# A fused attention and expert layer on one core: the context of four heads is turned by a DMA transpose instead of by TensorE

## The reference

```python
xn = _layernorm(x, axis=-1)
x = x + attention(xn, qkv_w, out_w, bias_p, bias_a, rope_freqs) + experts(xn, Wg, w1, w2)
```

```python
attn = jax.nn.softmax(scores + kb[None], axis=-1)
out = jnp.einsum('bhqk,bhkd->bhqd', attn, v)
out = out.transpose(0, 2, 1, 3).reshape(Bb, Ss, H * D)
return out @ out_w.T
```

## Time and profile before

| | before |
|---|---|
| median of 3 runs | 1443.87 us (1440.41 to 1444.68) |
| span of the profiled execution, first to last instruction | 1431.5 us |
| PE matmul busy | 1271.8 us (89%) |
| DVE busy | 1109.8 us (78%) |
| ACT busy | 1036.1 us (72%) |
| POOL busy | 696.1 us (49%) |
| mean granted TensorE clock | 0.945 of 2.4 GHz |

### The profile page before, as it was taken

How to read it: one execution, slowest core, us unless ns; L and a number is a source line. 1 busy time by engine, 2 the same in 40 slices (tenths; PEclk the granted TensorE clock), 3 DMA queues, 4 the chain that set the end, 5 groups by cost and what they waited for, 6 DMA issues and landing times.

```text
span 1431.5 us, 38280 instructions
## 1 busy us (share of the span) xinstructions
PE 1271.8 (89%) x13668; PEld 967.7 (68%) x13668; DVE 1109.8 (78%) x2166; ACT 1036.1 (72%) x1859; POOL 696.1 (49%) x536
## 2 busy tenths in 40 slices
PE   5622999995799999989998998999999999999996
PEld 5621888882477677767776776777677767777764
DVE  6873999973588887868886887788787868888885
ACT  3773888852688788768777787778688767877874
POOL 3064000004556666646655656566466646655600
PEclk8565999999899999999999999999999999999999
DMA  8554666621222223222312321132223212211220
GB/s 270 202 177 134 207 234 220 220 103 32 65 82 55 53 78 93 61 48 69 82 46 48 97 54 47 46 103 64 55 63 93 60 48 75 76 46 46 82 53 16
DMA packets 103602, 132.50 MB, mean 93 GB/s; under 512 B 17138, under 2 KB 89855, under 8 KB 103408
## 3 DMA queue, kind: packets, MB, share of 16 engines
q1 hardware_dynamic: 91136, 109.72, 26.4%
q0 software_dynamic: 4352, 12.41, 2.8%
q10 hardware_dynamic: 7920, 7.87, 1.7%
HBM read 58.79 MB, written 21.00 MB: 56 GB/s over the span
## 4 chain that ended last, share of the span: by engine, by line
PE 53%; ACT 7%; issue 7%; DVE 7%; SPq 1%; DVEq 1%; ACTq 0%; DMA 0%
PE ps_t L1294 13%; PE ps_x L1249 11%; PE ps_o L1319 8%; PE ps_s L1282 6%; PE ps_s L1283 6%; PE ps_x L1269 5%; ACT prob L1085 3%; DVE neg L1187 3%; PE ps_x L1259 3%; ACT ot_hi L1071 2%; DVE yacc L1172 1%; ACT pt_hi L1066 1%; SPq L963 1%; DVE yacc L1138 0%; DVE ctxt L1162 0%
## 5 line engine op out<-in xcount | busy, mean ns | idle before, releaser
L1144 DVE SCALAR_TENSOR_TENSOR pt_lo<-ps_t,pt_hi 128x1024 f16<-128x1024 f32 x256 | 312.6, 1221 | 155.2 <-ACT pt_hi L1066 155.2
L1187 DVE CUSTOM_DVE_ANT_0 neg<-ps_s,strips,score_scale 128x512 f32<-128x512 f32 x512 | 362.1, 743 | 31.9 <-PE ps_s L1283 28.1
L1085 ACT ACTIVATE prob<-neg,neg_max 128x512 f32<-128x512 f32 x512 | 362.9, 713 | 8.1 <-DVE neg_max L1187 8.1
L1066 ACT ACTIVATE pt_hi<-ps_t 128x1024 f16<-128x1024 f32 x256 | 262.0, 1023 | 113.4 <-PE ps_t L1294 113.0
L1014 POOL TENSOR_TENSOR parts<-rot,parts 128x1024 f16<-128x1024 f32 x62 | 132.2, 2134 | 307.5 <-ACT parts L1060 307.5
L1294 PE MATMUL ps_t<-ident,prob 128*128 128x128 f32 x2048 | 270.2, 274 | 3.8 <-ACT prob L1085 3.7
L1294 PEld LDWEIGHTS ps_t<-ident,prob 128*128 128x128 f32 x2048 | 236.5, 142 | 37.6 <-issue 9.3
L1282 PE MATMUL ps_s<-qk 128*128 128x512 f16 x512 | 198.1, 387 | 33.2 <-issue 18.4
L1319 PE MATMUL ps_o<-val_hi,pt_hi 128*128 128x64 f16 x2048 | 206.2, 193 | 14.5 <-DVE ctxt L1162 12.7
L1319 PE MATMUL ps_o<-val_hi,pt_lo 128*128 128x64 f16 x2048 | 206.2, 193 | 0.0
L1319 PE MATMUL ps_o<-val_lo,pt_hi 128*128 128x64 f16 x2048 | 206.2, 193 | 0.0
(11 more groups left out here) (186 smaller groups left out, 2518.9 us busy)
## 6 DMA issues: line engine op xcount, KB each, us to landing
raw<-in_L_ffn_w_dram SPq DMA_DIRECT2D x32, 1024.0 KB, 6.7
qk<-parts SPq DMA_DIRECT2D x512, 64.0 KB
kswap<-qk SPq DMA_DIRECT2D x64, 256.0 KB
xa<-in_L_attn_x_dram SPq DMA_DIRECT2D x8, 512.0 KB, 6.9
xt_dram<-xth SPq DMA_DIRECT2D x8, 512.0 KB, 5.1
slots_dram<-zeros SPq DMA_DIRECT2D x4, 1024.0 KB, 8.4
xa<-slots_dram SPq DMA_DIRECT2D x16, 256.0 KB, 5.1
expert_dram<-xa POOLq DMA_DIRECT2D x16, 256.0 KB, 6.3
```

The lines of the kernel that those rows point to most:

```text
L1066: nc.scalar.activation(pt[0][:, (l - 1) % 2].rearrange("p q k c -> p q (k c)"), ps_t[item % 2][:], ACT.Copy, scale=P_SCALE).then_inc(turne ...
L1085: nc.scalar.activation(prob[:, l % 2, q, :], neg[:, l % 2, q, :], ACT.Exp, bias=neg_max[:, 2 * (l % 2) + q:2 * (l % 2) + q + 1], scale=-1. ...
L1144: nc.vector.scalar_tensor_tensor(out=pt[1][:, (l - 1) % 2].rearrange("p q k c -> p q (k c)"), in0=ps_t[item % 2][:], scalar=P_SCALE, in1=p ...
L1187: nc.vector.tensor_tensor_reduce(neg[:, l % 2, q, :], ps_s[q][:], strips[:, h, start:start + S], score_scale[:, 0:1], 3.0e38, ALU.add, ALU ...
```

## The change

The context is no longer transposed by PE. `read_context` writes two heads (half a group) into a `ctxt` of half the size; ACT makes a float16 high part of it straight from SBUF (`context_hi`, at k = 2 and k = 6), DVE the low part (`context_lo`, at k = 3 and k = 7), both into `ctx_parts`. When both halves of a group are there, SP issues one DMA transpose of 128 x 2048 float16 values (512 KB, sixteen squares of 128 x 128) into `ot`. PE waits for it before the y fill at k = 6. In the program of SP `turn_context(b, j - 1)` comes before the `xcur` load and the `move` of the same j, and behind the `move` of the j before. To make room, `prod` shrinks to two slices, and POOL now writes two of the four products into `rot` and combines in place; the number and shapes of POOL's operations stay.

```diff
-        prod = sb("prod", [P, 4, S])
+        prod = sb("prod", [P, 2, S])
...
-        ctxt = sb("ctxt", [P, TPB, HG * D])
-        ot = [sb(f"ot_{n}", [P, 2, S], F16) for n in ("hi", "lo")]
+        ctxt = sb("ctxt", [P, TPB, P])
+        ctx_parts = sb("ctx_parts", [P, 2, 2, TPB, P], F16)
+        ot = sb("ot", [P, 2, 2, S], F16)
...
+            def turn_context(b, j):
+
+                group = 4 * b + j
+                wait(sp, filled, y_fills(b, j))
+                sp.sem_inc(went_on)
+                sp.wait_ge(ctx_lo, 2 * group + 2)
+                sp.sem_inc(went_on)
+                sp.dma_start_transpose(ot[:].rearrange("p a k (t c) -> p (a k t) c", t=TPB),
+                                       ctx_parts[:].rearrange("p a k t c -> p (a k t c)")).then_inc(ctx_turned, 16)
...
                 for j in range(4):
+                    if j or not is_first(b):
+                        turn_context(b, j - 1)
                     if j == 1 and not is_last(b):
...
+            turn_context(NB - 1, 3)
...
-                for i, (half, table) in enumerate(((0, cos), (1, sin), (0, sin), (1, cos))):
-                    nc.gpsimd.tensor_tensor(prod[:, i, :], proj[:, w, half, :], table[:], ALU.mult).then_inc(turned_parts, 1)
+                wait(pool, parts_lo, 2 * F - 1 + w)
+                for half, tables in enumerate(((cos, sin), (sin, cos))):
+                    nc.gpsimd.tensor_tensor(rot[:, w, half, :], proj[:, w, 0, :], tables[0][:], ALU.mult).then_inc(turned_parts, 1)
+                    nc.gpsimd.tensor_tensor(prod[:, half, :], proj[:, w, 1, :], tables[1][:], ALU.mult).then_inc(turned_parts, 1)
...
-            def ctx_hi(b, item):
-                act.wait_ge(turned, items(b, item))
-                nc.scalar.activation(ot[0][:], ps_t[item % 2][:], ACT.Copy, scale=1.0 / P_SCALE).then_inc(turned_hi, 1)
+            def context_hi(b, l):
+
+                unit = PAIRS // 4 * b + (l - 6) // 4
+                two = (l - 6) // 4 % 2
+                act.wait_ge(ctx_read, unit + 1)
+                if not two:
+                    wait(act, ctx_turned, 8 * unit)
+                act.sem_inc(went_on)
+                nc.scalar.activation(ctx_parts[:, 0, two], ctxt[:], ACT.Copy, scale=1.0 / P_SCALE).then_inc(ctx_hi, 1)
...
-                if k == 3 and not (is_first(b) and j == 0):
-                    ctx_hi(b, 9 * j + 4)
+                if l % 4 == 2 and not (is_first(b) and l == 2):
+                    context_hi(b, l)
...
+            def context_lo(b, l):
+
+                unit = PAIRS // 4 * b + (l - 6) // 4
+                two = (l - 6) // 4 % 2
+                dve.wait_ge(ctx_hi, unit + 1)
+                nc.vector.scalar_tensor_tensor(out=ctx_parts[:, 1, two], in0=ctxt[:], scalar=1.0 / P_SCALE, in1=ctx_parts[:, 0, two],
+                                               op0=ALU.mult, op1=ALU.subtract).then_inc(ctx_lo, 1)
...
-                if k == 3 and not (is_first(b) and j == 0):
-                    ctx_lo(b, 9 * j + 4)
+                if l % 4 == 3 and not (is_first(b) and l == 3):
+                    context_lo(b, l - 1)
...
-            def context_transposes(b, item, units):
-                wait(pe, turned_lo, items(b, item - 2))
-                pe.wait_ge(ctx_read, units)
-                for kt in range(2):
-                    for t in range(TPB):
-                        last = nc.tensor.transpose(ps_t[item % 2][:, kt, t * P:(t + 1) * P],
-                                                   ctxt[:, t, kt * P:(kt + 1) * P], ident[:])
-                last.then_inc(turned, 1)
...
                     if kind[0] == "y" and k == FILLS:
-                        pe.wait_ge(turned_lo, items(b, 9 * j + 4))
+                        pe.wait_ge(ctx_turned, 16 * (4 * b + j))
                     fill(kind, b, l, fills_before(b, l))
                 if l or not is_first(b):
                     transposes(b, l)
-                if k == 3 and not (is_first(b) and j == 0):
-                    context_transposes(b, 9 * j + 4, PAIRS // 4 * b + 2 * j)
```

More of the change, by code:

```diff
@@ L902, in fills_before, with pairs_turned, y_fills @@
             return n
[L904 to L912, removed]
+        def pairs_turned(b, l):
+            return PAIRS * b + l
+        def y_fills(b, j):
+            return fills_before(b, 8 * j + 8)
         def wait(eng, s, v):
@@ L1001, in turn, with rotate, low @@
                 wait(pool, turned_parts, done)
-                for i, (half, table) in enumerate(((0, cos), (1, sin), (0, sin), (1, cos))):
-                    nc.gpsimd.tensor_tensor(prod[:, i, :], proj[:, w, half, :], table[:], ALU.mult).then_inc(turned_parts, 1)
-                pool.wait_ge(turned_parts, done + 4)
-                wait(pool, parts_lo, 2 * F - 1 + w)
-                nc.gpsimd.tensor_tensor(rot[:, w, 0, :], prod[:, 0, :], prod[:, 1, :], ALU.subtract).then_inc(turned_parts, 1)
-                nc.gpsimd.tensor_tensor(rot[:, w, 1, :], prod[:, 2, :], prod[:, 3, :], ALU.add).then_inc(turned_parts, 1)
+                wait(pool, parts_lo, 2 * F - 1 + w)
+                for half, tables in enumerate(((cos, sin), (sin, cos))):
+                    nc.gpsimd.tensor_tensor(rot[:, w, half, :], proj[:, w, 0, :], tables[0][:], ALU.mult).then_inc(turned_parts, 1)
+                    nc.gpsimd.tensor_tensor(prod[:, half, :], proj[:, w, 1, :], tables[1][:], ALU.mult).then_inc(turned_parts, 1)
+            def rotate(F, w):
+                done = 6 * (2 * F + w)
+                pool.wait_ge(turned_parts, done + 4)
+                nc.gpsimd.tensor_tensor(rot[:, w, 0, :], rot[:, w, 0, :], prod[:, 0, :], ALU.subtract).then_inc(turned_parts, 1)
+                nc.gpsimd.tensor_tensor(rot[:, w, 1, :], rot[:, w, 1, :], prod[:, 1, :], ALU.add).then_inc(turned_parts, 1)
+            def low(F, w):
+                pool.wait_ge(parts_hi, 2 * F + w + 1)
+                nc.gpsimd.tensor_tensor(parts[:, 1, w], rot[:, w], parts[:, 0, w], ALU.subtract).then_inc(parts_lo, 1)
             def step(F, fills):
-                turn(F, 0, fills + 2)
-                turn(F, 1, fills + 4)
                 for w in range(2):
-                    pool.wait_ge(parts_hi, 2 * F + w + 1)
-                    nc.gpsimd.tensor_tensor(parts[:, 1, w], rot[:, w], parts[:, 0, w], ALU.subtract).then_inc(parts_lo, 1)
+                    multiply(F, w, fills + 2 * w + 2)
+                    rotate(F, w)
+                for w in range(2):
+                    low(F, w)
             def gather(b, j):
@@ L1083, in slot @@
                     if q == 0:
-                        wait(act, turned, items(b, pair_item(l - 1)))
+                        wait(act, turned, pairs_turned(b, l - 1))
                     nc.scalar.activation(prob[:, l % 2, q, :], neg[:, l % 2, q, :], ACT.Exp,
@@ L1119, in _ @@
             pair_hi(NB - 1, PAIRS)
-            ctx_hi(NB - 1, 37)
+            context_hi(NB - 1, PAIRS + 2)
         @block.vector
@@ L1157, in read_context @@
                 dve.wait_ge(pv_done, PAIRS * b + l - 2)
-                if not two:
-                    wait(dve, turned, items(b, 9 * (l // 8) + 4))
                 nc.vector.reciprocal(rsum[:], sums[:, two, :]).then_inc(chain, 1)
                 dve.wait_ge(chain, unit + 1)
-                nc.vector.tensor_tensor(ctxt[:, :, two * P:two * P + P].rearrange("p t (h d) -> p h t d", h=2),
+                nc.vector.tensor_tensor(ctxt[:].rearrange("p t (h d) -> p h t d", h=2),
                                         ps_o[:].rearrange("p (h t d) -> p h t d", h=2, t=TPB),
@@ L1288, in transposes @@
                 s = PAIRS * b + l
-                item = pair_item(l)
-                wait(pe, turned_lo, items(b, item - 2))
+                wait(pe, turned_lo, pairs_turned(b, l - 2))
                 for q in range(2):
@@ L1293, in transposes @@
                     for kt in range(TPB):
[L1294 removed]
+                        last = nc.tensor.transpose(ps_t[l % 2][:, q, kt * P:(kt + 1) * P],
                                                    prob[:, (l - 1) % 2, q, kt * P:(kt + 1) * P], ident[:])
[L1296 to L1304 removed]
                 last.then_inc(turned, 1)
```

28 lines of the change are left out of this document (10 added, 18 removed).

## The result

| | before | after |
|---|---|---|
| median of 20 runs | 1438.24 us (1432.27 to 1445.94) | 1448.78 us (1435.65 to 1458.50) |
| ratio, 95% interval | | 1.0055 (1.0029 to 1.0080) |
| span of the profiled execution | 1431.5 us | 1439.0 us |
| time of that execution | not listed | 1440.67 us |
| mean granted TensorE clock there | 0.945 | 0.956 |

The changed kernel is slower by 0.55%, about 8 us by the ratio. +57 us were forecast: the sign was right and the size seven times too large. The measured time lies inside the range of 1425 to 1680, and under the forecast's own range of 1460 to 1600.

A forecast was written before the change was run, and what follows sets the result against it. Attention was taken as bound by PE, busy 89%. Batches +41 us, clock +12 and tail +4 gave +57 on 1443.87, about 1500 us; own range 1460 to 1600, 8-in-10 range 1425 to 1680.

The forecast's parts named there:

- The direction: Whole kernel: the change makes it slower, chance 0.75.
- SP is still inside the `move`: SP's program: in groups 1 to 3 the transpose's issue is bound by SP, 1.1 us after the kswap issues end.
- the landing: Transpose into ot, from issue to landing: 6.5 us, taken between 4.3 and 9.0; landing of 5 to 10 us, chance 0.52.
- a short piece costs the same: Upper bound of landing: 256-byte pieces cost 49 ns like 1 KB packets, 6.3 us of moving, 9.0 us in all.
- my own sum: PE at slot 6, groups 0 to 3: -0.6, +3.7, +1.8, +0.2 us; +41 us over the stream, +57 with clock and tail.
- Rival A: Slot 6: the transpose lands like a plain copy, 1432 us, faster; sign turns at about 5.0 us landing; chance 0.25.
- Rivals B and C: B: squares issued one by one, 12.6 us landing, 1731 us, chance 0.15; C: squares strictly serial, about 2010 us, 0.08.
- The clock term: PE idle 6 us at slot 6 of group 1 lowers its clock: 1.5 us each in 8 groups, +12 us.
- The aftermath goes: Slots 4 and 5: 0.2 + 0.4 us extra behind the PE transposes vanish in each group; DVE's piece takes 0.75 us.
- The tail: At the end, ctxt done to first y fill grows from 4.3 to 8.1 us: +4 us.
- GpSimd's edit: POOL's four products wait for the previous step's low parts, which POOL itself finished earlier: zero cost.
- The base: Profiled span 1431.5 us plus 12.4 us around it gives the 1443.87 us median to which +57 us is added.

The follow-up runs named there:

- runs 1 and 3: Changed kernel with SP's transpose issued ahead of the kswap DMAs; the first also shortens ScalarE's wait, 1404.19 us; the second keeps it, 1401.97 us.
- run 9: Early transpose with old ScalarE wait, plus a second transpose of the 256 KB high half right behind it into an unread tile: 1408.64 us, one run.
- run 4: Changed kernel with a plain copy of the same 512 KB in place of the transpose: 1421.34 us, ratio 0.9897 to the kernel before.
- run 7: Changed kernel with the transpose ahead of kswap and the low part on GpSimd, 1/16384 multiplied in while ps_o is read: 1392.14 us, ratio 0.9667.
- run 8: Kernel before with only GpSimd's part of the change (prod of two slices, two products written into rot): 1441.78 us, ratio 1.0020.
- run 3: Changed kernel with the transpose ahead of the kswap DMAs, ScalarE's wait left as it was: 1401.97 us, ratio 0.9735 to the kernel before.

## Why the prediction was right and wrong, by its own steps

**The direction was right, and so was the place.** "SP is still inside the `move`" is what the trace shows. The transposes of the batch read above were forecast at 22.8 us of group 1 (948.9 - 926.1) and stood at 21.6 (949.32 - 927.70); in group 2 at 20.1 forecast and 19.3 measured. Between the `kswap` issues and the transpose SP took 0.4 us, where I had taken 1.1 from the row of `xcur`. Moving the transpose ahead of the wait for the 16 DMAs and of the two copies brought 45 us (runs 1 and 3). As forecast, groups 0 and 3 have little or no wait, and in batches 1 to 6 group 1 has the longest.

**The step that failed is the landing: 6.5 us forecast, 4.9 measured** at the median and in group 1, 3.7 where nothing else moves. It was the middle of 4.3 and 9.0 (6.65, taken as 6.5), and the 9.0 rested on "a short piece costs the same" as a packet of 1 KB, 49 ns, which gave 6.3 us of moving. The number of pieces was right: q1 has 66560 packets more than before (157696 against 91136), and the packet records of the trace hold 2048 of 256 bytes between the issue and the landing of each transpose. Their price was not. By the same records a 256-byte packet takes **18 ns** where the transpose lands in 3.7 us, and 18 to 28 ns beside other copies, 20 on average. 128 x 18 ns is 2.3 us of moving, which fits the 2.0 us of run 9, and not 6.3. The 3.7 us are 1.2 us to the first of these packets, 2.0 to the start of the last, and 0.5 to the landing; the 4.9 us of group 1 are 1.9, 2.5 and 0.5.

With 4.9 in my own sum the four groups give -1.5, +2.1, +0.2 and -1.4 us and the stream -3 us in place of +41. That alone is 44 of the 49 us that I was out. With it the whole sum, clock and a shorter tail included, is +11 us against +8 by the ratio. That it then comes so near is partly luck: it gives +8 us to batches 0 to 6 and +3 to batch 7, and they measured -2.9 and +10.0.

**Rival A was nearer.** It had the landing of a plain copy, 4.3 us, and gave 1432 us, with the sign turning at 5.0 us, or 4.3 if group 1 pays for the clock. At 4.9 us the time is indeed near the turn. The Trainium skill ("Advanced Engine Details and Errata", X-Bar Transpose) has transposes as fast as plain copies. The trace agrees only roughly: 4.9 against 4.1 us at the same place (run 4), and 3.7 against 2.8 in group 0. Rivals B and C, square by square, are out: all sixteen squares land in 4.9 us, and not in 12.6 or 21.6. The Trainium skill ("VectorE: DVE Perf Modes", The three transpose paths) has its figure for one square alone; an estimate of sixteen times that, 21 us, does not agree with the trace.

**The clock term was right in size, and not in where it falls.** I counted 1.5 us in each group 1, 12 us in all. Two groups 1 of the changed kernel show the price. In batches 4 and 6 the y fill begins behind the same 2.42 us of wait, at 954.30 and at 1218.21 us. The stretches from there to the next slot hold the same 44 matmuls:

```profile
954.30:958.85 4.55, 4.55 (x44) 4.05 (x45) 2.05 (x5) 0.54 (x1) 1.62 (x1) 0.62 0.27 98
1218.21:1221.09 2.88, 2.88 (x44) 2.75 (x45) 2.05 (x5) 0.49 (x1) 1.63 (x1) 1.00 0.36 129
```

(Length, busy time of PE, PEld, DVE, ACT, POOL, then the granted clock.) In the first the clock is at its lower level for most of the stretch, 0.62 on average, and the stretch is 1.67 us longer. So slot 6 of that group, 8.0 us, is 3.75 of work, 2.6 from when the y fill was due, and 1.67 for the clock. It fell in the groups 1 of batches 1, 2, 3, 4 and 7 and in group 2 of batch 7, 1.4 to 2.1 us each and 10.2 in all. It did not fall in group 1 of batch 0, where PE waited 3.38 us, nor in those of batches 5 and 6. I had taken the 3.86 us of the earlier trace rows as the idle time that it takes; here it came behind 2.05 us in one group and stayed away behind 3.38 in another, and what decides is open.

**"The aftermath goes" was wrong in groups 1 and 2.** I gave all of the 0.2 + 0.4 us of slots 4 and 5 back, and took 0.75 us for DVE's piece. The piece is 0.68 us alone, but 1.65 us in slot 3 of groups 1 and 2:

```profile
929.40 0.68 DVE L1191 SCALAR_TENSOR_TENSOR ctx_parts<-ctxt,ctx_parts 128x512 f16<-128x512 f32 x1
...
979.22 1.65 DVE L1191 SCALAR_TENSOR_TENSOR ctx_parts<-ctxt,ctx_parts 128x512 f16<-128x512 f32 x1
```

```profile
979.05 1.27 POOL L1018 TENSOR_TENSOR prod<-proj,sin 128x512 f32<-128x512 f32 x1
980.28 1.72 POOL L1017 TENSOR_TENSOR rot<-proj,sin 128x512 f32<-128x512 f32 x1
```

Slots 4 and 5 there last 4.1 and 4.17 us, more than before (3.95 and 4.16). In the changed kernel this cost little, since the wait at slot 6 swallowed most of it; behind an early transpose it is worth the 12 us of run 7. The old `ot_lo` read PSUM and was never held (1.22 to 1.23 us, all 32). The trace of before had the sign: the expert rows, with both tensors in SBUF, took 0.48 us at the median and 1.50 at the longest. The Trainium skill ("SBUF — State Buffer", SBUF: two separate sides) says that a VectorE operation with two SBUF inputs and a GpSimd operation that reads SBUF contend for a shared pair of ports, which is an exclusive lock. The trace agrees: the low part above begins inside a product of POOL and ends 0.55 us after it, and the next product takes 1.72 in place of 1.27 us. I had not looked.

**The tail** was forecast at +4 us. From `ctxt` done to the first y fill: 1422.72 + 0.69 = 1423.41 to 1428.66, 5.2 us against 4.3, so +1, since the transpose landed in 3.6 us there. **GpSimd's edit** at zero holds within the interval of run 8.

**Batch 7 was missed.** I counted its groups like the others. It lost 10.0 us, more than the whole span did (7.5), while batches 0 to 6 together gained 2.9 (the stretches above). In group 2 (5.6 us) its shorter slots meet the same late SP; that fits the timelines, and no run tested it alone. Why the transpose of its group 1 (4.2 us) took 6.2 us to land is open.

**The base.** I put 12.4 us around the span. The profiled execution of the changed kernel took 1440.67 us at a span of 1439.0, so 1.7 us lie around it. The 1431.5 us span of before was one of the shorter executions of its kernel, not the median less something.

## What to carry to other kernels

When an operation moves from an engine to a DMA, find where its issue lands in the issuing queue's program and what that queue is waiting for at that moment: here the same transfer, issued behind a wait and two copies instead of ahead of them, cost some 45 us: a gain of 2.7% (run 3) became a loss of 0.55%. Where one engine has two rows of waits, as PE and PEld here, see whether they are the same waits before adding them. Price a DMA of small pieces by its pieces only when a packet of that size is in the trace; a larger packet's time is an upper end and no price. And before giving VectorE an operation with all operands in SBUF, see what GpSimd does at that time; reading one operand from PSUM avoided the collision.

## What the runs showed of the hardware

- A DMA transpose of 128 x 2048 float16 values lands 3.7 us after its issue if nothing else moves (3.6 the shortest of 32), 4.9 us in the group where two copies of 256 KB stand right ahead, 7.7 at worst. A plain copy of the same bytes at the same places lands in 2.8 and 4.6 us. The transpose is moved in 2048 packets of 256 bytes, 18 ns each alone and up to 28 beside other traffic. A transpose of half the size right behind it landed 1.0 us later.
- A transpose holds the issuing queue: 1.4 to 1.7 us alone, 2.7 us at the median of all 32, up to 4.15, where the plain copy held it 0.48 us at the median.
- An operation of VectorE with all operands in SBUF can be held for a whole run of GpSimd operations and not for one only: 3.17 us for 128 x 8 elements, across three back-to-back products, until GpSimd had a gap of 0.07 us.
- A reciprocal of 128 x 8 in SBUF (0.19 us, never held in 64) is not held; the TENSOR_SCALAR of the same 128 x 8 is. The operations here that read PSUM were not held either: `ot_lo` (all 32) and the reading of `ps_o` in run 7 (all 128).
- Behind the same wait of PE, 2.42 us, the granted clock fell to an average of 0.62 in one group and stayed at 1.00 in another; where it fell, 2.88 us of work took 4.55.
